# Seven score products four periods sooner in a masked attention kernel on one Trainium2 core

## The reference

```python
h = relu(layernorm(x))                       # keys and values come from h
lQ = masked_x @ Wlq ; lK = h @ Wlk ; lV = h @ Wlv + blv
local_scores = where(adj, lQ @ lK.T * scale, -1e9)        # 4096 x 4096
global_scores, es = gQ @ gK.T * scale, masked_x @ Wes     # one column each
max_score = max(local_scores, global_scores, es)
le, ge, ee = exp(... - max_score)
denom = sum(le) + ge + ee
res = le / denom @ lV + ge / denom * gV + ee / denom * eV
out = x + maximum(res, masked_x)
```

## Time and profile before

| | |
|---|---|
| time before, median of 3 runs (lowest, highest) | 733.54 us (733.21, 733.62) |
| time of the profiled execution | 734.9 us |
| span of the profiled execution, first to last instruction | 733.0 us |
| PE busy in the span | 724.1 us (99%), 5248 matmuls |
| DVE / ACT / POOL busy | 563.7 (77%) / 531.9 (73%) / 432.4 us (59%) |
| mean granted TensorE clock | 0.998 of full speed |

### The profile page before, as it was taken

The page is one execution under the profiler, slowest core; times in us unless marked ns, Lnnn a source line. Parts: engine busy times, 40 slices in busy tenths (PEclk is TensorE's granted clock), DMA queues, the critical chain, the costliest instruction groups (busy, mean ns, idle before and its releaser), DMA issues.

```text
span 733.0 us, 15029 instructions
## 1 busy us (share of the span) xinstructions
PE 724.1 (99%) x5248; PEld 512.8 (70%) x5248; DVE 563.7 (77%) x1350; ACT 531.9 (73%) x706; POOL 432.4 (59%) x300
## 2 busy tenths in 40 slices
PE   9899999999999999999999999999999999999998
PEld 7667566676766776776767777676777767676787
DVE  6966788868787797878887887878878787876644
ACT  5863876786787677777868687678767777677690
POOL 4779489745555564556445555565556555654583
PEclk9999999999999999999999999999999999999999
DMA  7793586869789897987887798989878798887697
GB/s 243 169 197 61 105 168 160 169 144 204 144 182 168 166 177 142 203 154 176 170 172 158 152 203 142 192 156 178 174 167 163 151 208 148 179 171 174 118 179 166
DMA packets 364716, 121.93 MB, mean 166 GB/s; under 512 B 324832, under 2 KB 364640, under 8 KB 364640
## 3 DMA queue, kind: packets, MB, share of 16 engines
q1 hardware_dynamic: 364096, 120.44, 81.2%
q10 hardware_dynamic: 544, 0.52, 0.2%
HBM read 36.57 MB, written 4.19 MB: 56 GB/s over the span
## 4 chain that ended last, share of the span: by engine, by line
PE 88%; DMA 3%; ACT 2%; POOL 2%; DVE 2%; issue 2%; SPq 0%; DVEq 0%; ACTq 0%; POOLq 0%
PE ps_u L1107 14%; PE ps_u L1111 14%; PE ps_u L1109 14%; PE ps_x L1005 7%; PE ps_x L1004 7%; PE ps_x L1006 7%; PE ps_q L928 4%; PE ps_v L1004 3%; PE ps_v L1006 3%; PE ps_v L1005 3%; PE ps_w L1004 2%; PE ps_w L1005 2%; PE ps_w L1006 2%; PE ps_q L1173 1%; DMA hT<-v_rows 1%
## 5 line engine op out<-in xcount | busy, mean ns | idle before, releaser
L611 POOL TENSOR_TENSOR p_base<-s,p_base 128x1024 f16<-128x1024 f32 x112 | 242.3, 2163 | 227.2 <-ACT p_base L814 213.4
L1107 PE MATMUL ps_u<-v_rows,pT_base 128*128 128x256 f16 x968 | 263.8, 273 | 0.7 <-DMA pT_base<-bias 0.7
L1111 PE MATMUL ps_u<-v_rows,pT_base 128*128 128x256 f16 x968 | 263.8, 273 | 0.0
L1109 PE MATMUL ps_u<-v_rows,pT_base 128*128 128x256 f16 x968 | 263.8, 273 | 0.0
L777 ACT ACTIVATE bias<-adj,big 128x1024 f32<-128x1024 uint8 x127 | 156.5, 1237 | 130.1 <-DVE bmax L1476 126.1
L790 ACT ACTIVATE s<-s,negm,invc 128x1024 f32<-128x1024 f32 x128 | 157.0, 1226 | 6.9 <-DVE negm L1532 6.9
L814 ACT ACTIVATE p_base<-s 128x1024 f16<-128x1024 f32 x122 | 129.0, 1057 | 4.6 <-DMA pT_base<-p_base 0.8
L1107 PEld LDWEIGHTS ps_u<-v_rows,pT_base 128*128 128x128 f16 x968 | 94.7, 98 | 53.2 <-DMA pT_base<-bias 1.0
L1109 PEld LDWEIGHTS ps_u<-v_rows,pT_base 128*128 128x128 f16 x968 | 94.7, 98 | 52.1
L1476 DVE CUSTOM_DVE_ANT_0 s<-ps_x,bias 128x512 f32<-128x512 f32 x128 | 87.1, 685 | 49.6 <-PE ps_x L1006 46.1
L1111 PEld LDWEIGHTS ps_u<-v_rows,pT_base 128*128 128x128 f16 x968 | 94.7, 98 | 11.1
(11 more groups left out here) (242 smaller groups left out, 1266.7 us busy)
## 6 DMA issues: line engine op xcount, KB each, us to landing
adj<-adj SPq DMA_DIRECT2D x64, 256.0 KB, 3.2
pT_base<-p_base SPq DMA_TRANSPOSE x238, 3.3
s<-x SPq DMA_DIRECT2D x7, 512.0 KB, 5.1
f32q<-mx SPq DMA_DIRECT2D x14, 256.0 KB, 3.7
xm<-x SPq DMA_DIRECT2D x14, 256.0 KB, 3.1
xm<-mx SPq DMA_DIRECT2D x14, 256.0 KB, 3.5
out<-t_sb SPq DMA_DIRECT2D x14, 256.0 KB, 2.5
mxT_f<-mxT SPq DMA_DIRECT2D x4, 256.0 KB, 3.2
```

What stands on the lines that cost most here:

```text
L611: nc.gpsimd.tensor_tensor(p_rows(u)[:, 1], s32[:, p % NS, u % 2], p_rows(u)[:, 0], ALU.subtract).then_inc(s_plo, 1)
L1107: nc.tensor.matmul(acc, turn[:, 0, j], v_rows[:, kc, 0:D], start=opens, stop=False, skip_group_check=True)
L1109: nc.tensor.matmul(acc, turn[:, 0, j], v_rows[:, kc, D:2 * D], start=False, stop=False, skip_group_check=True)
L1111: done = nc.tensor.matmul(acc, turn[:, 1, j], v_rows[:, kc, 0:D], start=False, stop=end, skip_group_check=True)
```

## The change

`PC` goes from 12 to 8: periods 8 to 11 (the third query pair) use seven products. `LOW_AT` = 8 takes the place of `PC - 2` in `low_on_dve`, so units 6 to 9 of `p_low` go from DVE to POOL. On POOL the third pair's `q_sums` and `q_low` come ahead of the key forms of group 2, and the key forms are spread otherwise over periods 4 to 10. The two pairs of T3 sums move from periods 10 and 12 to 6 and 8, and their ACT step gets two more waits. DVE's periods 8 to 11 take the order of the seven-product loop.

```diff
-    PC = 12
+    PC = 8
+    LOW_AT = 8
         def low_on_dve(u):
-            return u // 2 + LAG_E < PC - 2
+            return u // 2 + LAG_E < LOW_AT
@@ POOL, loop over p
                 if live:
                     p_low(u)
-                if p % NG == 2 and 2 <= n < NP:
+                if p == 6:
+                    q_low(2)
+                    keys_t1(2)
+                    keys_t2(2)
+                elif p % NG == 2 and 2 <= n < NP:
                     q_low(n)
...
                 if live:
                     p_low(u + 1)
+                if p == 7:
+                    keys_t4(2)
                 if p % NG == 3 and QH <= (p + 5) // NG < NP:
                     mx_low((p + 5) // NG)
...
-                if p in (4, 6, 8):
-                    keys_t1(p // 2 - 1)
-                    keys_t2(p // 2 - 1)
-                if p in (5, 7, 9):
-                    keys_t4((p - 3) // 2)
+                if p == 4:
+                    keys_t1(1)
+                    keys_t2(1)
+                    keys_t4(1)
+                if p == 8:
+                    keys_t1(3)
+                if p == 9:
+                    keys_t2(3)
+                if p == 10:
+                    keys_t4(3)
@@ ACT
             def keys_t3_high(g):
                 act.wait_ge(s_t3sum, g + 1)
+                act.wait_ge(s_t1, g + 1)
+                act.wait_ge(s_p7, PC - NG + g + 1)
@@ PE
             def keys_t3_sum(g):
                 if g < 2:
-                    pe.wait_ge(s_qf, PC - 3)
+                    pe.wait_ge(s_qf, 7)
                 else:
-                    pe.wait_ge(s_c2, 2)
+                    pe.wait_ge(s_t3, 2)
             def es_values(n):
-                if n == 0:
-                    pe.wait_ge(s_t3, 2)
@@ DVE, loop over p: of the branch p < PC
-                    if p == 8:
-                        row_max(1)
...
-                    if p == 9:
-                        wev_low()
-                    if step == 1 and p >= 9:
-                        weights((p - 9) // NG)
...
@@ DVE, of the branch p >= PC
-                    ended = done < NP - 1
+                    ended = 0 <= done < NP - 1
...
+                    if p == 9:
+                        wev_low()
```

## The result

The changed kernel takes 744.27 us (median of 4 runs, 743.75 to 744.41), the kernel before on the same chip 733.43 (4 runs, 733.21 to 733.62): 10.84 us slower, ratio 1.014, 95% interval 1.0128 to 1.0152. The forecast was +7.2 us with a range up to 743.6. The sign and both named waits are there; the size is not.

The account below looks back on a forecast made before the run. PE, busy 99% of the span, was taken as the bound, by its matmul count and its waits. -2.6 + 8.8 + 1.0 = +7.2 us took the median from 733.54 to 740.7, range 738.0 to 743.6.

Parts of the forecast that it names:

- Term A: PE's matmuls: four periods go from 8 products to 7, 0.65 us each; -2.6 us.
- Term B: PE's waits at p1(8) and project(3) together, with the projection starting at 122.0; +8.8 us, bounds 6.9 to 10.3.
- the lower bound: For both waits together, 6.9 us: p_high(7) not later than before, and hand-overs at nothing.
- The first wait: PE at p1(8) waits for DVE's out22(7), delayed by 1.28 us of T3 work; 4.3 us, bounds 3.0 to 5.3.
- The second wait: PE at project(3) waits for the fourth T3 form, through p_high(7), p_low(7) and keys_t1(3); 4.5 us more.
- Clock behind the second wait: Rival: PE's clock halves for some 3.4 us after the project(3) wait, costing 1.7 us; 742.4, chance 0.27.
- Term C: Periods 9 to 12: POOL's queue delays p_low(10), so p5(11) waits for out12(10); +1.0 us, bounds 0 to 2.0.
- More is late behind it: Rival: full queues behind period 8 bring a further wait of 2 to 3 us; 743.5, chance 0.11.
- The moves taken at nothing: Third pair's transposed queries, mx_low(3), SP's transposes of units 6 to 9, and ACT's delayed steps: no cost each.
- If waits stand behind period 12, I underrated what is late: Sign against the forecast in the profile: PE waits behind period 12 would mean lateness was underrated; no size given.

Follow-up runs that it names:

- values_first: Changed kernel with 14 of period 8's 16 p_times_v steps, p5(8) and p2(8) ahead of p1(8) on PE; 746.73 us.
- values_t1: Changed kernel with period 8's value steps, p5 and p2 ahead of p1(8) on PE, and keys_t1(3) ahead of p_low(6) on POOL; 739.93 us.
- before_pause: Kernel before the change with four reductions, read by nobody, added on DVE at the start of period 13; 735.61 us.
- dense_wait: Changed kernel with 12 unused products of ones on PE in its wait ahead of p1(8); 744.25 us.
- t2_early: Changed kernel with keys_t2(3) on POOL directly behind keys_t1(3) in period 8 in place of period 9; 743.41 us.
- gates_t3: Changed kernel with period 8's value steps ahead of p1(8), POOL's key forms reordered over periods 7 and 8, wev_low in period 13, subtractions starting period 9; 738.05 us.
- subs_late: Changed kernel with the two subtractions on gv_b and bev_b moved on DVE from period 7 to period 9; 743.09 us.

## Why the prediction was right or wrong

- **Term A (-2.6)**: right. 12 matmuls fewer.
- **Term B (+8.8, bounds 6.9 to 10.3)**: right in its mechanism, 9.7 measured. Both gates exist and they are the operations that were named: `out22(7)` and the fourth T3 form. values_first shows that the second gate stands by itself, at 121.09; values_t1, with `keys_t1(3)` ahead of `p_low(6)` and `(7)` and nothing else changed, has it at 115.81, so that place on POOL is what sets it. (The two items named for the lower bound, 1.28 and 0.2, give 7.3 and not 6.9.)
- **The first wait (4.3, bounds 3.0 to 5.3)**: 6.6, outside. PE could have been there at 101.16, forecast 102.98, and `out22(7)` ended at 107.61, forecast 107.25. That the latter is so close is luck. The clock fall in the profile of before had moved both by 1.8 us, as before_pause shows, and cancels in their difference. What was mis-sized is the 1.28 us of T3 work as the only lateness of DVE: from before_pause to the changed kernel `out22(7)` came 3.45 us later (104.16 to 107.61). DVE's blocks of period 6 were 0.8 us later already, and behind the T3 work its operations met POOL's at other moments. The largest are an operation on two elements, 1.13 for 0.16, and a `p_low`, 1.64 for 1.23; before_pause, then the changed kernel:

```profile
101.18 0.16 DVE L1458 TENSOR_SCALAR mpow<-mcl 128x2 int32<-128x2 int32 x1
...
101.45 1.23 DVE L1542 TENSOR_TENSOR p_base<-s,p_base 128x1024 f16<-128x1024 f32 x1
```

```profile
103.25 1.13 DVE L1468 TENSOR_SCALAR mpow<-mcl 128x2 int32<-128x2 int32 x1
...
104.49 1.64 DVE L1552 TENSOR_TENSOR p_base<-s,p_base 128x1024 f16<-128x1024 f32 x1
...
106.92 0.69 DVE L1488 CUSTOM_DVE_ANT_0 s<-ps_x,bias 128x512 f32<-128x512 f32 x1
```

- **The second wait (4.5)**: 0.3, and yet the gate was within 1 us of the forecast: 121.07 for 122.0, with `p_high(7)` done at 111.83 (112.85) and `keys_t1(3)` at 119.5 (120.5). Here too luck helped: against before_pause `p_high(7)` came 2.06 us later and not 1.28, which makes 0.8 of the 0.9 us that term B lacked, and the fall had hidden it. The first wait and the half clock behind it took the second wait's place, which the prediction allowed for. dense_wait bears out that the fall itself cost nothing: with half of it gone, the projection started at the same 121.07.
- **Clock behind the second wait (rival, 0.27)**: did not happen in the changed kernel; it happens in values_first, for 2.5 us, when the wait of the projection is the long one.
- **Term C (+1.0, bounds 0 to 2.0)**: the step that failed. 3.5 us in four waits. I took `p_low(10)` as late through POOL's own queue (`keys_t2(3)` and `q_sums(3)` ahead of it) and counted one wait at the place where I had followed the chain to. t2_early shows that path to be wrong: with `keys_t2(3)` gone from it POOL idled for 3.47 us, for ACT, and `out11(10)` and `p5(11)` waited as before (1.48, 0.91). In the changed kernel's trace ACT is late since its mask waits for `out12(9)`. And a lateness comes back in later pairs, at periods 15 and 19: before_pause shows that in the old kernel, 2.1 us for 2.8 us of DVE. Where the lateness in periods 8 to 10 comes from stays open. The waits at 107 and 121 are an obvious source, but the later waits at `p5` don't go by them: 3.5 us behind 6.7 us of waits in the changed kernel, 2.9 behind 9.5 in values_first, 3.9 behind 0.8 and then 2.2 in gates_t3. What period 9 itself now holds on DVE is another, and no run parts the two. "If waits stand behind period 12, I underrated what is late" is what came.
- **More is late behind it (rival, 0.11, 743.5)**: this is what happened, and the chance was too small. It named `out11(11)` and `out11(12)`, held by POOL's queue; the waits stand at `p5` behind `out12`.
- **The moves taken at nothing**: right, the new queries, `mx_low(3)` and the transposes made no wait. But one thing that the change did not move was part of the first gate: the subtractions in period 7. Without them it came 3.65 us sooner (subs_late).

So +7.2 went to +10.8 by +0.9 in term B and +2.5 in term C; 0.2 is left over.

## What to carry to other kernels

Two gates in a row on the bounding engine must be costed by the later one, and an edit that opens only one of them may show nothing or be a loss (-1.3, +2.5, and -4.3 for both). A lateness of an engine that isn't the bound can come back as small waits periods later: a place where a DVE pause of 2.8 us was "hidden" still cost 2.1. Work put ahead of a chain on DVE can delay its end by more than its own length, as other operations then meet POOL's (1.28 us forecast, 3.45 found). A disturbance early in the profile, such as a clock fall, moves PE's arrival and the gates alike, so it cancels in a wait as long as both are taken from one execution. Before moving a small step into an idle slot, see what runs on POOL in that slot, not how long the step takes elsewhere.

## What the hardware showed that I had not expected

In the rows below, DVE instructions with two inputs in SBUF that began during one of POOL's ended shortly behind it, whatever their own size. In the rows of DVE and POOL ahead of `p5(11)`, POOL's operations end at 141.62 + 1.89 = 143.51 and 143.46 + 2.31 = 145.77, and DVE's two `side_rows` at 143.79 and 146.05, each 0.28 behind; POOL idle, the step takes 0.53. Even operations on two elements do so, in gates_t3 (timeline of DVE, and of POOL):

```profile
112.75 1.01 DVE L1554 TENSOR_TENSOR mrow<-mloc,invc 128x2 f32<-128x2 f32 x1
113.79 1.08 DVE L1556 TENSOR_TENSOR mtop<-mrow,ges 128x2 f32<-128x2 f32 x1
```

```profile
109.52 4.21 POOL L615 TENSOR_TENSOR p_base<-s,p_base 128x1024 f16<-128x1024 f32 x2
113.70 1.15 POOL L548 TENSOR_TENSOR tw<-hT,tw 128x512 f32<-128x512 f16 x1
```

DVE's end at 113.76 and 114.87, POOL's at 113.73 and 114.85. With POOL idle the same two take 0.16 each in the changed kernel. In these rows the price of such an operation is the rest of POOL's instruction, not its own time. One that began first was not held: the subtraction at 96.19 in the changed kernel took 0.41, with POOL's next instruction starting at 96.22. The Trainium skill (SBUF — State Buffer, Who interferes with whom) says that the shared port pair is locked for a whole instruction by the one that came first; these rows agree, and they show that a chain of tiny operations can pay it each time. An operation on two elements with one input was held too: `mpow` at 103.25 above ended at 104.38, POOL's instruction from 103.19 at 104.35.

The clock fell during a wait of PE of 6.6 us though `keep_busy` filled 2.8 us of it with dense products (dense_wait), but for half as long, 3.4 us and not 6.8; and with a wait of 8.8 us it was at half for 10.2 us in all (values_first). Shorter waits went either way: 3.11 us in subs_late brought a fall of 3.4 us, of which 2.9 us lay on work, while 3.40 in the same run and 3.52 and 2.85 in values_t1 brought none. The length of the wait alone does not tell.
